# Attention sums spread by a matmul and inverted in the values' layout, in a conv-attention-lookup block on one core

## The chip, the cores and the metric

The kernel runs on one core of a Trainium2 chip. The metric is the time on the device of one execution in microseconds (us): of the kernel before, the median of three runs.

## The reference, cut to what matters

`x` is a (2, 128, 16, 16) tensor. It is group-normalised and goes through a decaying scan over its 128 channels; the sum with `x` is read as 2 x 256 tokens of 128 features. Then comes attention with 8 heads of 16 dimensions and a recency bias, and last a table-like integer lookup that tests some channels of each token and adds one-hot vectors:

```python
x = x + _L0_conv_ref(_gn(x), ...)
t = _to_tokens(x)                                  # 2 x 256 x 128
# attention
qkv = jnp.einsum('bsh,oh->bso', _ln_t(t), w_qkv)
attn = jnp.einsum('bhqd,bhkd->bhqk', q, k) / math.sqrt(hd)
bias = jnp.where(pos <= 0, pos * math.log(0.9), 0.0)
attn = jax.nn.softmax(attn + bias, axis=-1)
out = jnp.einsum('bhqk,bhkd->bqhd', attn, v).reshape(batch, seq_len, hidden)
t = t + jnp.einsum('bsh,oh->bso', out, w_out) + b_out
# lookup: bits of the normalised token select a shift of an 8-bit value
t = t + _L1_ffn_ref(_ln_t(t))
```

## The kernel before

Every engine has one program written out by hand; each step waits for named semaphores and raises one. There is no scheduler: an engine runs its steps strictly in the order of the code, so the calls at the ends of the `scalar`, `vector` and `tensor` blocks and the loops of the `gpsimd` block set the order.

Up to about 16 us the normalisation, the scan and the first projections run. Then comes attention. Its 2 batches x 8 heads are 16 heads, in four groups `g` of four (`HG`), two groups to a batch. A head goes through these steps:

- `scores_by_query(h)` (TensorE): scores with queries on the partitions, 2 products of 256 columns, into one of two PSUM buffers `s1_ps`. `largest(h)` (VectorE) takes each query's largest, `L741`; the next use of that buffer, by head `h + 2`, waits for it. Behind the fourth head of a group, `largest` also writes the negative maxima as two fp16 parts, `mparts` (`L748`, `L749`).
- `shift_rows(g)` (TensorE) transposes `mparts`; `even_shifts(g)` (ScalarE, `L477`) and `odd_shifts(g)` (VectorE, `L664`) copy the rows into spare rows of `qT`, so that the next product includes the shift.
- `scores_by_key(h)` (TensorE, `L975`, `L977`): the scores again with keys on the partitions, shifted, and `exponentials(c)` (ScalarE, `L496`) for two heads at once, 1,024 columns.
- `values(g, t)` (TensorE, `L994`): the product with `v_aug`. The output `pv_ps[g]` is 128 x 256 in fp32: each head has a block of 32 partitions (`VW`), 16 dimensions, then the sum of the exponentials (a column of ones in `v_aug`), then zeros; the 256 columns are queries. The four heads use four column blocks of the array. `pv_ps` of groups 0 to 2 is one PSUM bank, so the products of the next group wait until that bank has been read.
- `by_query(g)` (VectorE, `L671`) transposes 32x32 blocks, so that a query's sum is one column in each block of 32; `invert(g)` (`L675`) takes the reciprocal of 8 columns; GpSimd multiplies (`L344`, `L352`); `by_dim(g)` (VectorE, `L679`) transposes back into `oT`.
- `project(b)` (TensorE, `L1010`): four fp32 products of a batch's two groups with `woutT`; `residual(b)` and `token_stats(b)` (VectorE, `L685` to `L692`) add and take statistics; `token_scale` (ScalarE), `find_channels`, `look_up`, `one_hots` (VectorE, `L698` to `L732`), the fields `hot` (GpSimd) and `plus_normalised` (ScalarE) form the lookup, and `output(b)` transposes.

`keep_warm` issues products of zeros (`L814`) that nothing reads. GpSimd also writes the constants in its spare time, then `t1b` and `second_lows(t)` (`L307`): copies that the transposes of the stacks of queries and keys (`transpose_stacks`, `L916`) wait for.

Of the kernel before, what the change touches and what calls it, by code (L numbers as in the profile page):

```python
# [15 lines left out]
P = 128  # L16
# [18 lines left out]
WARM_X, WARM_Z, WARM_SCAN, WARM_MAX, WARM_PV, WARM_OUT = 9, 1, 5, 2, 8, 7  # L35
# [5 lines left out]
def conv_attn_ffn(nc, x, log_A, dt_w, dt_b, ln_w, ln_b, w_qkv, w_out, b_out, out):  # L41
# [3 lines left out]
    with ExitStack() as ctx:  # L45
# [199 lines left out]
        def _(pool):  # L245
# [84 lines left out]
            link(pool.tensor_scalar(ident2[:], ident16[:], 2.0, 0.0, ALU.mult, ALU.add), s=s_consts)  # L330

# [10 lines left out]
            for g in range(NG - 1):  # L342
                pool.wait_ge(s_rsum, g + 1)
                pool.tensor_tensor(on[:, g, :, :], pvq[:, g, :, :],  # L344
                                   rsum[:, g, :].unsqueeze(2).broadcast_to([P, HW // VW, VW]), ALU.mult)\
                    .then_inc(s_on, 1)

            for b in range(B):
                ts = slice(HALVES * b, HALVES * (b + 1))
                if b == 1:  # L350
                    pool.wait_ge(s_rsum, NG)
                    pool.tensor_tensor(on[:, NG - 1, :, :], pvq[:, NG - 1, :, :],  # L352
                                       rsum[:, NG - 1, :].unsqueeze(2).broadcast_to([P, HW // VW, VW]), ALU.mult)\
                        .then_inc(s_on, 1)
                pool.wait_ge(s_frs, b + 1)
                link(pool.tensor_scalar(neg_frs[:, ts], frs[:, ts], -1.0, 0.0, ALU.mult, ALU.add),
                     pool.tensor_scalar(one_frs[:, ts], frs[:, ts], 1.0, 0.0, ALU.add, ALU.add))
                pool.tensor_tensor(neg_fm[:, ts], fmv[:, ts, 0], neg_frs[:, ts], ALU.mult).then_inc(s_nfm, 1)
                pool.wait_ge(s_above, b + 1)
                link(pool.tensor_scalar(lift[:, ts], above[:, ts, SHL], 0.5, 0.5, ALU.mult, ALU.add))  # L360
                pool.tensor_tensor(hot[:, ts, :, :], hot_at[:].unsqueeze(1).broadcast_to([P, HALVES, 2, D]),
                                   lift[:, ts].unsqueeze(2).unsqueeze(3).broadcast_to([P, HALVES, 2, D]), ALU.mult)\
                    .then_inc(s_hot, 1)
# [445 lines left out]
        def _(pe):  # L809
# [171 lines left out]
            def values(g, t):  # L981

                b = g // 2
                if g == NG - 1:
                    pe.wait_ge(s_mre, NG)
                    pe.wait_ge(s_mro, NG)
                elif g > 0:
                    pe.wait_ge(s_pvq, g)
                else:
                    pe.wait_ge(s_odd, NG - 1)  # L990
                    pe.wait_ge(s_even, NG - 1)
                pe.wait_ge(s_exp, 2 * g + 2)
                for j in range(HG):
# [124 lines left out]
```

## Time and profile before

| | |
|---|---|
| runs | 54.54, 54.62, 56.0 us; median 54.62 |
| the profiled execution | 54.57 us, of it 52.8 us span |
| busy in the span | TensorE 41.4 us (78%), VectorE 41.0 (78%), ScalarE 28.7 (54%), GpSimd 22.1 (42%) |
| granted TensorE clock | 1.00 |
| the chain that ended last | TensorE 51% of the span, VectorE 24%, ScalarE 13%, waiting for nothing shown 5%, GpSimd 1% |

The span runs from the first to the last instruction; 1.8 us of the time lie outside it. Busy shares average over stages of different kinds. The chain is followed back from the last instruction, at each step to what released it, so its shares tell in which engine's hands the end lay.

### The profile page before, as it was taken

The numbers are of one execution on the slowest core, as the hardware profiler recorded it, in microseconds if no ns is written. First come the engines' busy times: TensorE is split into PE (matmuls) and PEld (weight loads), VectorE is DVE, ScalarE is ACT, GpSimd is POOL, SyncE is SP. The second block draws the span as 40 slices with busy tenths as digits, with TensorE's granted clock in tenths as the row PEclk, the third lists the DMA queues.
The fourth block names the chain that finished last, engine by engine and source line by source line (L and its number), as shares of the span: only waits on it lengthen the run. The fifth ranks groups of instructions, "written<-read, shape, count | busy, mean of one in ns | idle before, by whom it ended". The sixth has DMA issues, their size and how long they took to land.

```text
span 52.8 us, 1024 instructions
## 1 busy us (share of the span) xinstructions
PE 41.4 (78%) x317; PEld 26.1 (49%) x317; DVE 41.0 (78%) x136; ACT 28.7 (54%) x63; POOL 22.1 (42%) x62
## 2 busy tenths in 40 slices
PE   0999999199993989717994997899996399996710
PEld 0331988073521765315861594389664246841500
DVE  2699577859868279999979999998899964599620
ACT  3500476397392599806999239609839910045120
POOL 4788323099999886993000004021009304007000
PEclk9999999999999999999999999999999999999999
DMA  0482300000000000000000000000000000002002
GB/s 0 88 283 50 33 3 0 0 0 0 0 0 0 6 0 0 6 19 0 0 0 0 0 0 0 0 0 0 0 12 0 0 0 0 0 0 86 13 0 99
DMA packets 1565, 0.92 MB, mean 17 GB/s; under 512 B 404, under 2 KB 1560, under 8 KB 1560
## 3 DMA queue, kind: packets, MB, share of 16 engines
q1 hardware_dynamic: 1104, 0.79, 5.0%
q10 hardware_dynamic: 456, 0.08, 1.5%
q8 instruction: 2, 0.03, 0.3%
q14 instruction: 3, 0.02, 0.2%
HBM read 0.60 MB, written 0.26 MB: 16 GB/s over the span
## 4 chain that ended last, share of the span: by engine, by line
PE 51%; DVE 24%; ACT 13%; issue 5%; POOL 1%; DVEq 0%; ACTq 0%
PE ps L814 13%; PE ps L994 8%; ACT probs L496 8%; DVE negmax L741 6%; PE ps L975 5%; PE ps L1010 4%; PE ps L977 3%; PE ps L916 3%; PE ps L944 3%; DVE stacks L660 3%; PE ps L840 2%; PE ps L894 2%; ACT parts L435 2%; DVE xt L627 1%; DVE parts L648 1%
## 5 line engine op out<-in xcount | busy, mean ns | idle before, releaser
L814 PE MATMUL ps<-warm 128*128 128x512 bf16 x35 | 10.8, 444 | 1.3 <-DVE warm L541 1.3
L741 DVE TENSOR_REDUCE negmax<-ps 128x2 f32<-128x512 f32 x16 | 10.7, 674 | 0.7 <-PE ps L944 0.6
L496 ACT ACTIVATE probs<-ps 128x1024 f32<-128x1024 f32 x8 | 8.0, 1021 | 3.9 <-PE ps L977 3.9
L344 POOL TENSOR_TENSOR on<-pvq,rsum 128x256 f32<-128x256 f32 x3 | 1.8, 615 | 14.1 <-DVE rsum L675 14.1
L975 PE MATMUL ps<-stacks 128*128 128x256 f16 x32 | 7.0, 273 | 0.0
L977 PE MATMUL ps<-qmk,ident 128*128 128x256 f16 (+1 forms) x32 | 6.6, 246 | 0.0
L814 PEld LDWEIGHTS ps<-warm 128*128 128x128 bf16 x35 | 3.6, 109 | 5.7 <-issue 2.6
L944 PE MATMUL ps<-stacks 128*128 128x256 f16 x32 | 6.0, 273 | 0.5 <-DVE negmax L741 0.3
L994 PE MATMUL ps<-probs,v_aug 128*32 128x256 f32 x64 | 4.3, 384 | 1.7 <-ACT probs L496 1.5
L944 PEld LDWEIGHTS ps<-stacks 128*128 128x128 f16 x32 | 2.4, 97 | 2.4 <-issue 1.6
L975 PEld LDWEIGHTS ps<-stacks 128*128 128x128 f16 x32 | 3.1, 98 | 0.8 <-ACT stacks L477 0.4
L994 PEld LDWEIGHTS ps<-probs,v_aug 128*32 128x32 f32 x64 | 1.9, 109 | 3.1 <-issue 2.0
L977 PEld LDWEIGHTS ps<-qmk,ident 128*128 128x128 f16 x32 | 3.1, 98 | 0.2
L483 ACT ACTIVATE fln<-fmv 128x2 f32<-128x2 f32 x2 | 0.4, 204 | 5.1 <-DVE fmv L692 5.1
L473 ACT COPY stacks<-ps 64x1024 f16<-64x1024 f16 x3 | 3.0, 1007 | 0.3 <-PE ps L916 0.3
L894 PE MATMUL ps<-wT,xtT 128*128 128x384 f32 x8 | 3.0, 496 | 0.1
L958 PE MATMUL ps<-ident,mparts 128*128 128x128 f16 x8 | 1.1, 224 | 2.1 <-DVE mparts L749 2.1
L916 PE MATMUL ps<-ident,parts 128*128 128x128 f16 x32 | 2.3, 219 | 0.3 <-POOL parts L307 0.3
L679 DVE STREAM_TRANSPOSE oT<-on 128x256 f32<-128x256 f32 x4 | 1.8, 443 | 0.9 <-POOL on L352 0.7
L477 ACT COPY stacks<-ps 64x512 f16<-64x512 f16 x4 | 2.3, 580 | 0.3 <-PE ps L958 0.2
L544 DVE MEMSET stacks<- 64x1024 uint32 x2 | 1.8, 912 | 0.5 <-issue 0.5
L916 PEld LDWEIGHTS ps<-ident,parts 128*128 128x128 f16 x32 | 1.8, 97 | 0.8 <-POOL parts L307 0.5
(157 smaller groups left out, 92.5 us busy)
## 6 DMA issues: line engine op xcount, KB each, us to landing
x_sb<-in_x_dram SPq DMA_DIRECT2D x1, 256.0 KB, 2.9
out_dram<-y_sb SPq DMA_DIRECT2D x2, 128.0 KB, 1.7
wqkv_sb<-in_L_attn_w_qkv_dram SPq DMA_DIRECT2D x1, 192.0 KB, 3.0
wout_sb<-in_L_attn_w_out_dram SPq DMA_DIRECT2D x1, 64.0 KB, 3.3
bout_bc<-in_L_attn_b_out_dram ACTq DMA_DIRECT2D x1, 64.0 KB, 4.1
params<-in_L_conv_ln_w_dram ACTq DMA_DIRECT2D x1, 1.0 KB
params<-in_L_conv_ln_b_dram ACTq DMA_DIRECT2D x1, 1.0 KB
params<-in_L_conv_dt_w_dram ACTq DMA_DIRECT2D x1, 0.5 KB
```

What stands on the lines that cost most here:

```text
L473: act.copy(group_stacks(g, 0)[0:P // 2], stacks_ps[g][0:P // 2]).then_inc(s_even, 1)
L477: act.copy(qT.rearrange("p (a e) t -> p a e t", e=2)[P // 2:P, 2 * (g % 2):2 * (g % 2) + 2, 0, HW * (g // 2):HW * (g // 2 + 1)], mT_ps[P / ...
L496: act.activation(probs[:, 2 * c:2 * c + 2, :, :].rearrange("p h k q -> p (h k q)"), s2_ps[c % 2].rearrange("p a n -> p (a n)"), ACT.Exp, s ...
L741: dve.tensor_reduce(negmax[:, g, :, quadrant], s1_ps[h % 2].rearrange("p (q k) -> p q k", q=HALVES), AX_X, ALU.max, negate=True).then_inc( ...
L814: pe.matmul(ps[:, bank, :], warm[:, 0:P], warm[:], start=True, stop=True)
L894: pe.matmul(qkv_ps[:, t, 0:3 * P], xtT[:, P * t:P * (t + 1)], wT[:, 0:3, :].rearrange("p k h -> p (k h)"), start=True, stop=True).then_inc ...
L916: last = pe.transpose(stacks_ps[g][:, o, a, P * t:P * (t + 1)], parts[:, 2 * b + t, o, h:h + 2, :, :] .rearrange("p h i d -> p (h i d)"), ...
L944: last = pe.matmul(s1_ps[h % 2][:, HW * t:HW * (t + 1)], qT[:, e, HW * b + P * t:HW * b + P * (t + 1)], kT[:, e, HW * b:HW * (b + 1)], sta ...
L975: pe.matmul(dst, kT[:, e, HW * b + P * t:HW * b + P * (t + 1)], qT[:, e, HW * b:HW * (b + 1)], start=True, stop=False)
L977: last = pe.matmul(dst[:, P * t:HW], ident16[:], qmk[:, 0:HW - P * t], start=False, stop=True)
L994: last = pe.matmul(pv_ps[g][VW * j:VW * (j + 1), :], v_aug[:, 2 * b + t, HG * (g % 2) + j, :], probs[:, HG * g + j, t, :], start=(t == 0), ...
L1010: last = pe.matmul(proj_ps[b][:, t, :], oT[:, 2 * b + g, P * t:P * (t + 1)], woutT[:, g, :], start=(g == 0), stop=(g == 1))
```

## The change

The sum of a head's exponentials stays where the values product leaves it, in row 16 of the head's block of 32 partitions. A group's 128 x 256 block is copied to SBUF (`copy_values`: ScalarE for groups 0, 1 and 3, VectorE for group 2). A new step of TensorE, `spread_sums(g)`, multiplies it with a constant matrix `spread` that copies row 16 of each block onto its 32 rows; the result `sums_ps[g]` has the sum of each query under every value. VectorE takes the reciprocal of all 256 columns (`normalise`), GpSimd multiplies (VectorE for group 3), and the product is `oT` without a transpose. `spread` is written by two more instructions of GpSimd among its constants.

Beside that: `odd_shifts(1)` and `(2)` go from VectorE to ScalarE; `values(g, c)` goes by pairs of heads and not by halves of the keys, so that it can start on one exponential; `project(1)` is in two halves around `spread_sums(3)`, and the residual and the statistics of the last batch go tile by tile; eight fillers (`WARM_PV`) in front of `project(1)` go; `token_scale(0)` stands behind the last copy of values, and `hot_fields(0)` on GpSimd ahead of group 2's product. Queries 12 to 14 stand ahead of values of group 1.

```diff
-WARM_X, WARM_Z, WARM_SCAN, WARM_MAX, WARM_PV, WARM_OUT = 9, 1, 5, 2, 8, 7
+WARM_X, WARM_Z, WARM_SCAN, WARM_MAX, WARM_OUT = 9, 1, 5, 2, 7
...
-        pvq = sb("pvq", [P, NG, HW // VW, VW])
-        rsum = sb("rsum", [P, NG, HW // VW])
-        on = sb("on", [P, NG, HW // VW, VW])
+        pv_sb = sb("pv_sb", [P, NG, HW])
+        rsum = sb("rsum", [P, NG, HW])
+        spread = sb("spread", [P, P])
...
+        sums_ps = [ps[:, bank, HW:2 * HW] for bank in (6, 6, 6, 7)]
...
+            link(pool.memset(spread[:], 0.0), s=s_consts)
+            blocks = spread[:].rearrange("p (j w) -> p j w", w=VW)
+            link(pool.affine_select(out=blocks, in_=blocks, compare_op=ALU.not_equal, fill=1.0, base=-HD,
+                                    pattern=[[-VW, HG], [0, VW]], channel_multiplier=1), s=s_consts)
...
+            for g in range(NG - 1):
+                if g == NG - 2:
+                    hot_fields(0)
+                pool.wait_ge(s_rsum, g + 1)
+                pool.tensor_tensor(oT[:, g, :], pv_sb[:, g, :], rsum[:, g, :], ALU.mult).then_inc(s_oT, 1)
...
+            def copy_values(g):
+                act.wait_ge(s_pv, g + 1)
+                act.copy(pv_sb[:, g, :], pv_ps[g]).then_inc(s_pvc, 1)
...
             for g in range(1, NG):
                 even_shifts(g)
-                if g == NG - 1:
-                    token_scale(0)
+                if g < NG - 1:
+                    odd_shifts(g)
+                    copy_values(g - 1)
                 exponentials(2 * g)
                 exponentials(2 * g + 1)
+            copy_values(NG - 1)
+            token_scale(0)
...
-            def by_query(g):
-
-                dve.wait_ge(s_pv, g + 1)
-                dve.transpose(pvq[:, g, :, :].rearrange("p a w -> p (a w)"), pv_ps[g]).then_inc(s_pvq, 1)
-
-            def invert(g):
-                dve.wait_ge(s_pvq, g + 1)
-                dve.reciprocal(rsum[:, g, :], pvq[:, g, :, HD]).then_inc(s_rsum, 1)
-
-            def by_dim(g):
-                dve.wait_ge(s_on, g + 1)
-                dve.transpose(oT[:, g, :], on[:, g, :, :].rearrange("p a w -> p (a w)")).then_inc(s_oT, 1)
+            def copy_values():
+                dve.wait_ge(s_pv, NG - 1)
+                dve.tensor_copy(pv_sb[:, NG - 2, :], pv_ps[NG - 2]).then_inc(s_pvc2, 1)
+
+            def normalise(g):
+                dve.wait_ge(s_sums, g + 1)
+                dve.reciprocal(rsum[:, g, :], sums_ps[g]).then_inc(s_rsum, 1)
+                if g == NG - 1:
+                    dve.wait_ge(s_rsum, g + 1)
+                    dve.wait_ge(s_oT, g)
+                    dve.tensor_tensor(oT[:, g, :], pv_sb[:, g, :], rsum[:, g, :], ALU.mult).then_inc(s_oT, 1)
...
             def residual(b):
 
+                if b == 1:
+                    for t in tiles(1):
+                        dve.wait_ge(s_proj, t)
+                        dve.wait_ge(s_t1b, t + 1)
+                        dve.tensor_tensor(t2[:, t, :], proj_ps[1][:, t - HALVES, :], t1b[:, t, :], ALU.add)\
+                           .then_inc(s_t2, 1)
+                        dve.wait_ge(s_t2, t)
+                        dve.bn_stats(fst[:, t, :], t2[:, t, :]).then_inc(s_fst, 1)
...
+            def values(g, c):
...
+                pe.wait_ge(s_exp, 2 * g + c + 1)
+                for t in range(HALVES):
+                    for j in range(2 * c, 2 * c + 2):
+                        last = pe.matmul(pv_ps[g][VW * j:VW * (j + 1), :],
+                                         v_aug[:, 2 * b + t, HG * (g % 2) + j, :], probs[:, HG * g + j, t, :],
+                                         start=(t == 0), stop=(t == HALVES - 1))
...
+            def spread_sums(g):
+                if g == NG - 2:
+                    pe.wait_ge(s_pvc2, 1)
                 else:
+                    pe.wait_ge(s_pvc, min(g + 1, NG - 1))
+                if g == 0:
+                    pe.wait_ge(s_consts, 12)
+                elif g < NG - 1:
+                    pe.wait_ge(s_rsum, g)
+                pe.matmul(sums_ps[g], spread[:], pv_sb[:, g, :], start=True, stop=True).then_inc(s_sums, 1)
...
+            def project(b, groups=range(2)):
...
+                                     start=(g == 0), stop=(g == 1), skip_group_check=True)
+                    if b == 1 and g == 1:
+                        last.then_inc(s_proj, 1)
+                if b == 0:
+                    last.then_inc(s_proj, 1)
...
+            scores_by_query(12)
+            shift_rows(2)
+            scores_by_query(13)
+            scores_by_query(14)
+            values(1, 0)
+            values(1, 1)
+            scores_by_query(15)
+            scores_by_key(8)
+            scores_by_key(9)
...
             values(2, 0)
-            values(2, 1)
             for h in range(HG * (NG - 1), HG * NG):
                 scores_by_key(h)
+            values(2, 1)
             values(3, 0)
+            spread_sums(2)
             values(3, 1)
-            keep_warm(WARM_PV, 2)
-            project(1)
+            project(1, [0])
+            spread_sums(3)
+            project(1, [1])
             output(0)
```

GpSimd, the last of its constants. Names are those of tensors, written<-read; in brackets the semaphores that a row waits for. Before:

```order
L330 TENSOR_SCALAR ident2<-ident16 128x128 [waits consts]
L332 MEMSET eq2 128x288 [waits consts]
L338 TENSOR_TENSOR t1b<-t1,bout_bc 128x128 [waits t1_ready,bout_in]
L338 TENSOR_TENSOR t1b<-t1,bout_bc 128x128
L338 TENSOR_TENSOR t1b<-t1,bout_bc 128x128 [waits t1_ready]
L338 TENSOR_TENSOR t1b<-t1,bout_bc 128x128
L307 COPY parts<-parts 128x2x8x16 [waits lo_ready] x2
```

After:

```order
L333 TENSOR_SCALAR ident2<-ident16 128x128 [waits consts]
L334 MEMSET spread 128x128 [waits consts]
L336 AFFINE_SELECT spread<-spread 128x128 [waits consts]
L339 MEMSET eq2 128x288 [waits consts]
L345 TENSOR_TENSOR t1b<-t1,bout_bc 128x128 [waits t1_ready,bout_in]
L345 TENSOR_TENSOR t1b<-t1,bout_bc 128x128
L345 TENSOR_TENSOR t1b<-t1,bout_bc 128x128 [waits t1_ready]
L345 TENSOR_TENSOR t1b<-t1,bout_bc 128x128
L310 COPY parts<-parts 128x2x8x16 [waits lo_ready] x2
```

Two instructions for `spread` stand between `ident2` and `eq2`, ahead of `t1b` and of the copies of `second_lows(2)` and `(3)`.

VectorE, from `largest(9)` on; `pvq` is what `by_query` writes, and each `TENSOR_REDUCE` is a `largest`. Before:

```order
L741 TENSOR_REDUCE negmax<-ps 128x2 [waits s1_done]
L671 STREAM_TRANSPOSE pvq<-ps 128x256 [waits pv_done]
L741 TENSOR_REDUCE negmax<-ps 128x2 [waits s1_done]
L675 RECIPROCAL rsum<-pvq 128x8 [waits pvq_ready]
L741 TENSOR_REDUCE negmax<-ps 128x2 [waits s1_done]
L748 TENSOR_SCALAR mparts<-negmax 128x8 [waits max_ready]
L749 SCALAR_TENSOR_TENSOR mparts<-negmax,mparts 128x8 [waits dve_step]
L741 TENSOR_REDUCE negmax<-ps 128x2 [waits s1_done]
L679 STREAM_TRANSPOSE oT<-on 128x256 [waits on_ready]
L664 COPY stacks<-ps 64x2x256 [waits mT_done]
L741 TENSOR_REDUCE negmax<-ps 128x2 [waits s1_done]
L671 STREAM_TRANSPOSE pvq<-ps 128x256 [waits pv_done]
```

After, from `largest(8)` on (x4: four in a row):

```order
L772 TENSOR_REDUCE negmax<-ps 128x2 [waits s1_done] x4
L779 TENSOR_SCALAR mparts<-negmax 128x8 [waits max_ready]
L780 SCALAR_TENSOR_TENSOR mparts<-negmax,mparts 128x8 [waits dve_step]
L694 RECIPROCAL rsum<-ps 128x256 [waits sums_spread]
L772 TENSOR_REDUCE negmax<-ps 128x2 [waits s1_done] x4
L779 TENSOR_SCALAR mparts<-negmax 128x8 [waits max_ready]
L780 SCALAR_TENSOR_TENSOR mparts<-negmax,mparts 128x8 [waits dve_step]
L694 RECIPROCAL rsum<-ps 128x256 [waits sums_spread]
L684 COPY stacks<-ps 64x2x256 [waits mT_done]
```

The transposes are gone. `normalise(0)` stands between `mparts` of group 2 and `largest(12)`, `normalise(1)` behind `mparts` of group 3, and the third odd shift behind it.

TensorE, from the last values product of group 3 to the end of `project(1)`. Before:

```order
L994 MATMUL ps<-probs,v_aug 32x256 [waits exp_done,odd_shifts,even_shifts]
L994 MATMUL ps<-probs,v_aug 32x256 x3
L994 MATMUL ps<-probs,v_aug 32x256 [waits exp_done,odd_shifts,even_shifts]
L994 MATMUL ps<-probs,v_aug 32x256 x3
L814 MATMUL ps<-warm 128x512 x8
L1010 MATMUL ps<-woutT,oT 128x128 [waits oT_ready,t2_ready,max_ready]
L1010 MATMUL ps<-woutT,oT 128x128 [waits oT_ready] x3
```

After, with `values(2, 1)` ahead of `values(3, 0)` no longer shown:

```order
L1018 MATMUL ps<-probs,v_aug 32x256 [waits exp_done,odd_shifts,even_shifts]
L1018 MATMUL ps<-probs,v_aug 32x256 x3
L1033 MATMUL ps<-pv_sb,spread 128x256 [waits sums_inverted,third_values_copied]
L1018 MATMUL ps<-probs,v_aug 32x256 [waits exp_done]
L1018 MATMUL ps<-probs,v_aug 32x256 x3
L1045 MATMUL ps<-woutT,oT 128x128 [waits oT_ready,t2_ready,max_ready]
L1045 MATMUL ps<-woutT,oT 128x128 [waits oT_ready]
L1033 MATMUL ps<-pv_sb,spread 128x256 [waits values_copied]
L1045 MATMUL ps<-woutT,oT 128x128 [waits oT_ready,t2_ready,max_ready]
L1045 MATMUL ps<-woutT,oT 128x128 [waits oT_ready]
```

The fillers are gone; `spread_sums(2)` stands ahead of `values(3, 1)`, and `spread_sums(3)` between the halves of `project(1)`.

## Rows read from the trace of the kernel before

**Rows 1.** Windows: stretch, length; busy us of PE, PEld, DVE, ACT, POOL; PEclk, DMA, GB/s.
```profile
29.00:37.50 8.50, 8.00 (x87) 5.82 (x88) 8.04 (x20) 4.93 (x6) 1.23 (x2) 1.00 0.00 0
37.50:41.80 4.30, 2.95 (x37) 1.95 (x38) 4.06 (x18) 3.16 (x7) 1.74 (x6) 1.00 0.02 4
```

**Rows 2.** The chain that ended last, in order of time: start us, us, work.
```profile
23.90 0.41 POOL parts L307
...
24.35 0.62 PE ps L916 x8
```

**Rows 3.** Timeline of GpSimd: start us, us, work, [idle before <-releaser].
```profile
0.80 0.20 POOL L256 MEMSET ident<- 128x128 f32 x1 [0.29 <-POOLq L1104]
...
2.03 0.53 POOL L262 TENSOR_SCALAR_AFFINE_SELECT group_avg<-group_avg 128x128 f32<-128x128 f32 x1
...
2.62 0.52 POOL L264 TENSOR_SCALAR_AFFINE_SELECT group_avg<-group_avg 128x128 f32<-128x128 f32 x1
...
23.42 0.88 POOL L307 COPY parts<-parts 128x256 f16<-128x256 f16 x2
```

**Rows 4.** Groups of VectorE by line: count | busy us, mean ns | idle before.
```profile
L741 DVE TENSOR_REDUCE negmax<-ps 128x2 f32<-128x512 f32 x16 | 10.7, 674 | 0.7 <-PE ps L944 0.6
...
L671 DVE STREAM_TRANSPOSE pvq<-ps 128x256 f32<-128x256 f32 x4 | 1.8, 445 | 0.5 <-PE ps L994 0.5
...
L685 DVE TENSOR_TENSOR t<-ps,t1b 128x256 f32<-128x256 f32 x2 | 0.8, 425 | 0.6 <-PE ps L1010 0.5
...
L675 DVE RECIPROCAL rsum<-pvq 128x8 f32<-128x8 f32 x4 | 0.8, 196 | 0.1
...
L721 DVE TENSOR_TENSOR mask<-mask_at,active 128x4 uint32<-128x4 f32 x2 | 0.3, 154 | 0.0
```

**Rows 5.** Timeline of TensorE.
```profile
19.21 1.46 PE L894 MATMUL ps<-wT,xtT 128*128 128x384 f32 x4
...
29.02 1.07 PE L994 MATMUL ps<-probs,v_aug 128*32 128x256 f32 x16 [0.22 <-DVE stacks L660]
...
30.02 0.39 PE L944 MATMUL ps<-stacks 128*128 128x256 f16 x2
...
31.02 0.38 PE L944 MATMUL ps<-stacks 128*128 128x256 f16 x2
...
31.23 0.27 PE L975 MATMUL ps<-stacks 128*128 128x256 f16 x1
...
32.00 0.38 PE L944 MATMUL ps<-stacks 128*128 128x256 f16 x2
...
32.71 0.29 PE L958 MATMUL ps<-ident,mparts 128*128 128x128 f16 x2 [0.33 <-DVE mparts L749]
...
36.35 1.11 PE L1010 MATMUL ps<-woutT,oT 128*128 128x128 f32 x8
```

**Rows 6.** Timeline of ScalarE.
```profile
12.40 0.37 ACT L424 COPY wT<-ps 128x256 f32<-128x256 f32 x1
...
31.21 2.01 ACT L496 ACTIVATE probs<-ps 128x1024 f32<-128x1024 f32 x2 [1.81 <-PE ps L977]
...
33.25 0.58 ACT L477 COPY stacks<-ps 64x512 f16<-64x512 f16 x1
```

**Rows 7.** Timeline of several engines in the tail.
```profile
43.75 0.61 POOL L352 TENSOR_TENSOR on<-pvq,rsum 128x256 f32<-128x256 f32 x1 [2.23 <-DVE rsum L675]
...
45.65 0.42 DVE L685 TENSOR_TENSOR t<-ps,t1b 128x256 f32<-128x256 f32 x1 [0.50 <-PE ps L1010]
...
46.62 1.69 PE L814 MATMUL ps<-warm 128*128 128x512 bf16 x7
...
46.63 0.25 DVE L692 BATCH_NORM_AGGREGATE fmv<-fst 128x2 f32<-128x6 f32 x2
...
48.74 0.17 DVE L719 SCALAR_TENSOR_TENSOR idx<-first,flip 128x6 uint32<-128x6 uint32 x1
...
48.83 0.78 PE L1022 MATMUL ps<-ident,t 128*128 128x128 f32 x4 [0.53 <-ACT t L490]
```

More of the change, by code:

```diff
@@ L340, in _, with hot_fields @@
             second_lows(3)
[L342 to L348, printed above, removed]
-                ts = slice(HALVES * b, HALVES * (b + 1))
[L350 to L358, printed above, removed]
+            def hot_fields(b):
+                ts = slice(HALVES * b, HALVES * (b + 1))
                 pool.wait_ge(s_above, b + 1)
@@ L363, in _ @@
                     .then_inc(s_hot, 1)
+            for g in range(NG - 1):
[3 more added lines that the diff above has]
+                pool.tensor_tensor(oT[:, g, :], pv_sb[:, g, :], rsum[:, g, :], ALU.mult).then_inc(s_oT, 1)
+            for b in range(B):
+                ts = slice(HALVES * b, HALVES * (b + 1))
+                pool.wait_ge(s_frs, b + 1)
+                link(pool.tensor_scalar(neg_frs[:, ts], frs[:, ts], -1.0, 0.0, ALU.mult, ALU.add),
+                     pool.tensor_scalar(one_frs[:, ts], frs[:, ts], 1.0, 0.0, ALU.add, ALU.add))
+                pool.tensor_tensor(neg_fm[:, ts], fmv[:, ts, 0], neg_frs[:, ts], ALU.mult).then_inc(s_nfm, 1)
+                if b == 1:
+                    hot_fields(b)
         @block.scalar
@@ L979, in scores_by_key @@
                     last.then_inc(s_s2, 1)
-            def values(g, t):
+            def values(g, c):
                 b = g // 2
[L984 to L988, printed above, removed]
-                else:
[L990 to L993, printed above, removed]
-                    last = pe.matmul(pv_ps[g][VW * j:VW * (j + 1), :],
-                                     v_aug[:, 2 * b + t, HG * (g % 2) + j, :], probs[:, HG * g + j, t, :],
-                                     start=(t == 0), stop=(t == HALVES - 1))
-                if t == HALVES - 1:
-                    last.then_inc(s_pv, 1)
@@ L1000, in project @@
-            def project(b):
+                if c == 0:
+                    if g == NG - 1:
+                        pe.wait_ge(s_mre, NG)
+                        pe.wait_ge(s_mro, NG)
+                    elif g > 0:
+                        pe.wait_ge(s_pvc, g)
+                    else:
+                        pe.wait_ge(s_odd, NG - 1)
+                        pe.wait_ge(s_even, NG - 1)
+                pe.wait_ge(s_exp, 2 * g + c + 1)
[4 more added lines that the diff above has]
+                                         start=(t == 0), stop=(t == HALVES - 1))
@@ L1001, in project @@
+            def project(b, groups=range(2)):
                 if b == 0:
                     pe.wait_ge(s_max, B * HEADS - 1)
-                    steps = [(t, g) for t in range(HALVES) for g in range(2)]
+                    steps = [(t, g) for t in range(HALVES) for g in groups]
                 else:
@@ L1006, in project @@
                     pe.wait_ge(s_t2, 1)
-                    steps = [(t, g) for g in range(2) for t in range(HALVES)]
+                    steps = [(t, g) for g in groups for t in range(HALVES)]
                 for t, g in steps:
@@ L1010, in project @@
                     last = pe.matmul(proj_ps[b][:, t, :], oT[:, 2 * b + g, P * t:P * (t + 1)], woutT[:, g, :],
-                                     start=(g == 0), stop=(g == 1))
-                last.then_inc(s_proj, 1)
+                                     start=(g == 0), stop=(g == 1), skip_group_check=True)
+                    if b == 1 and g == 1:
+                        last.then_inc(s_proj, 1)
+                if b == 0:
+                    last.then_inc(s_proj, 1)
             def output(b):
```

67 lines of the change are left out of this document (37 added, 30 removed).

## The prediction

> **What bounds the kernel now.** I read the chain that ended last first, since shares of busy time say little here: VectorE and TensorE are both over nine tenths busy from 29 to 37.5 us [rows 1]. The chain [rows 2] shows at 23.90 us that GpSimd's copy in `second_lows(3)` releases TensorE's transposes of the third stack group at 24.35, and that everything up to the values products of the first group at 29.02 [rows 5] hangs on them. From there TensorE's own queue carries the chain, broken by two exponentials per group. So three things can move the end: what delays GpSimd before 24 us, what lengthens TensorE's queue from 29 us on, and the row of steps behind the last exponential: values, sums, division, projection, residual. The last is serial: no engine has other work that could be late instead.
>
> The profiled execution took 54.57 us, 52.8 of them span; the median is 54.62, so sums against 54.57 hold for it.
>
> **Part 1: the matrix `spread` on GpSimd.** A memset and an `affine_select` are put ahead of the memset of `eq2`, in a queue with no gap up to `second_lows(2)` at 23.42 [rows 3]. Likes of both stand at the start: a 128x128 memset 0.20 us and a two-dimensional select 0.53, each with a 0.06 gap before the next [rows 3]: 0.85 us. `second_lows(2)` starts at 24.27, and (3) right behind it ends at 25.15 instead of 24.31. TensorE waits for exactly that, so 0.83 of it reach 29.02: **values(0) starts at 29.85**. Nothing between hides it: TensorE already sat idle before 24.35, and VectorE and ScalarE next wait for TensorE. If one dimension makes the select cheaper, 0.6 remains.
>
> **Part 2: what a 256-column reciprocal costs.** This is the term that decides. Before, `invert` takes 8 columns in 196 ns on average, while a VectorE operation on 4 columns takes 154 [rows 4], thus some 150 fixed. Two readings: the surplus is fixed, and 256 columns cost what the addition of 256 from PSUM costs, 0.43 us [rows 4]; or it is per column, (196-150)/8 = 5.75 ns, and 256 columns cost 0.15 + 1.47 = **1.62 us**. I take the second: at one column per cycle 8 columns add under 10 ns to an operation, as 4 against 256 show ((425-154)/252 = 1.1 ns each), and nothing else about this instruction, whose input is a column taken from each block of 32, explains five times that. Its ends are 0.43 and, with the slowest surplus I can read from the row's rounding, 1.8.
>
> The Trainium skill ("VectorE: DVE Perf Modes", First, the fixed hardware budget) says that reciprocal is an iterative divide "with a repeat count of 8". At eight steps for every column one reciprocal would be an estimated 2.3 us and the sum 63.5; the row of 8 columns is about 20 ns too short for that, so the rule is taken for its sign, and the row for the size.
>
> **Part 3: 29 to 39 us.** Steps of TensorE's queue by start-to-start [rows 5]: values of one group 1.00 us, one query score 0.21, a pair of key scores 0.77, the row transposes 0.12 (their 0.29 less the drain of 0.17, which a pair of queries shows as 0.38 less 0.21). `spread_sums` is an fp32 product of 256 columns; two fp32 projections of 384 columns took 1.46, 1.29 without the drain [rows 5], 1.68 ns a column, so 0.43 each. ScalarE gets odd shifts (as its even shifts, 0.58) and copies of values (as a 128x256 copy, 0.37) [rows 6]: per group 2.0 + 0.58x2 + 0.37 = 3.5 of a period over 4.3 us; it keeps up and costs nothing here. The DVE transposes go, 0.445 each [rows 4], from beside that queue.
>
> From 29.85: values 30.85, query 10, keys 4 and 5 31.85, query 11 32.06, spread_sums(0) 32.49, keys 6 and 7 33.26, query 12 33.48, shift and query 13 33.82. Query 14 writes over what `largest(12)` reads, and on VectorE `normalise(0)` stands ahead of `largest(12)`: behind `mparts` (33.3) it runs to 34.9, `largest(12)` takes 0.67 [rows 4] to 35.5. TensorE stands from 33.82 to 35.52, where its longest wait before was 0.33 [rows 5]. Behind query 14: values(1) 36.75, query 15 36.97, keys 37.74, spread_sums(1) 38.17, keys **38.94**. Before, this point is at 36.35 [rows 5]: 2.6 later, of which 0.83 are part 1, 0.86 the two spreads, 1.17 the reciprocal over the short reading, 0.5 the queries moved together, less 0.8 of old waits. `normalise(1)` waits for `largest(15)` and `mparts` (38.3), ends at 39.97; GpSimd multiplies for 0.61 [rows 7] to 40.65; three of the four products of project(0) wait for that and end at 41.40, residual(0) starts at 41.57.
>
> **Part 4: the tail.** values(2,0) uses two of the four column blocks: four products run at once in the 1.00 of [rows 5], here two, so it takes as long as a whole group. Keys 12 to 15 end at 43.94, values(2,1) and (3,0) together near 45.3. VectorE's residual(0) to the start of look_up is 3.09 long (45.65 to 48.74 for the second batch [rows 7]), then copies group 2's values, 0.42: 45.07. The rest is serial: spread_sums(2) to 45.73, drained 45.9; reciprocal to 47.5; GpSimd's product 48.2; project(1,[0]) 0.44, 48.7; spread_sums(3) 49.13, drained 49.3 (ScalarE's copy was done long before); reciprocal 50.95; VectorE's product about 0.42, 51.4; first half of project(1,[1]) 51.75. The halves save about 0.2: the first addition starts while the second product runs, but two additions and two statistics with a wait between each take 0.1 more than the joined ones. The first addition starts at 51.77, and the statistics end at 53.15 where before they end at 46.88 [rows 7]: **6.2 us later**. One-hots(0), token_scale(0) and the fields of GpSimd lie in the reciprocals' shadow; what stands behind the statistics is unchanged. The eight fillers that go stood in a wait of VectorE and GpSimd and cost nothing before. Sum: 54.57 + 6.2 = **60.8 us**.
>
> **Rivals.**
> (a) *The reciprocal is one column per cycle.* Four times 1.19 less, all four on the chain: 54.57 + 6.2 - 4.8 = 56.0 us, 55.0 to 57.0 with part 1 at 0.6, and with 0.4 more if half groups of values don't overlap. For it: the surplus is read from 8 columns only. Against: the size of that surplus. It decides at about 0.6 us a reciprocal.
> (b) *In between:* part of the surplus is fixed, the reciprocal costs 0.7 to 1.2: 57.2 to 59.4.
> (c) *Faster: VectorE sets the pace and is relieved.* It is 8.04 of 8.50 us busy from 29 to 37.5 [rows 1] and TensorE waits for its `mparts` at 32.71 [rows 5]. Four transposes (1.8) go there and two short reciprocals (0.9) come, and the tail loses two transposes (0.9) and 0.2 by the halves: -2.0, with part 1's 0.85 left -1.2: 53.4 us. It needs the short reciprocal and ScalarE, not VectorE, to be unimportant; against it, TensorE is 8.00 of 8.50 busy in the same stretch and gets two more products.
> (d) *TensorE's clock falls.* From 46 to 51.4 us it would have 1.9 us of work. The granted clock stayed at 1.00 (2.4 GHz) where it was busy 2.95 of 4.30 us [rows 1]; nothing as sparse is in the trace. At 1.2 GHz output(0) and the seven fillers, 45.65 to 48.31 now [rows 7], take 5.3 instead of 2.7, end at 57.2, and hold output(1), due at 48.83 + 6.2 = 55.0: 62.9 us. The skill ("TensorE: Matmul & The Clock Gate", What's actually happening) has the slow clock as the default that activity releases; no row here shows it fall.
>
> **How the numbers follow.** My forecast with its own range 59.5 to 62.3: 0.47; (d) 0.10; (b) 0.10; (a) 0.26; (c) 0.07. The likeliest is 60.8. From 55.6 to 63.0 leaves out (c), the lower part of (a) and little above: under 2 in 10. A change within 2% (about what can be told from none) ends at 55.7: about 0.4 of (a) and a little of (c), 0.13; faster 0.06; slower 0.81.
>
> **What would show each step.** Part 1: TensorE's third stack transposes at 25.2, not 24.35. Part 2: RECIPROCAL 128x256 at 1.6 us. Part 3: TensorE idle 1.7 before query 14, released by `largest(12)`; spread products 0.43 apart. Part 4: VectorE's two last reciprocals on the chain, and gaps of 2 us on TensorE before each half of project(1). I am wrong if the reciprocal is under 0.6 us, and too low if TensorE's clock drops.

## The result, and the profile after

| | before | after |
|---|---|---|
| runs | 54.54, 54.62, 56.0, 56.4; median 55.31 us | 65.01, 65.2, 65.74, 65.76; median 65.47 us |
| the profiled execution | 54.57 us | 65.76 us |
| its span | 52.8 us | 64.0 us |
| granted TensorE clock | 1.00 | 0.92 |

The ratio is 1.199, interval 1.184 to 1.213: slower, by 4.7 us more than the 60.8 that were forecast and 2.5 above 63.0, the top of the range. Some executions of every kernel here, before's 56.0 and 56.4 among them, are 1 us or more longer, and where one was profiled, attention mostly began 0.9 to 1.7 us later; the ratio leaves them out. The two profiled executions are 11.2 us apart, and these 11.2 are what the text accounts for.

The page of the kernel after, first the clock in 40 slices of 1.6 us, then the group of the new reciprocal (count | busy us, mean ns | idle before):

```profile
PEclk9999999999999999999999955899999998555599
...
L694 DVE RECIPROCAL rsum<-ps 128x256 f32<-128x256 f32 x4 | 7.0, 1756 | 3.5 <-PE ps L1033 3.5
```

Both halves of the story stand here. A 256-column reciprocal takes 1.756 us, above the 1.62 of the forecast. And the clock is at half in two places, which it never was in the profiled execution of before. The windows, in the columns of [rows 1]:

```profile
29.50:33.60 4.10, 4.08 (x44) 2.91 (x44) 3.56 (x7) 2.83 (x5) 0.00 (x0) 1.00 0.00 0
33.60:36.80 3.20, 1.43 (x20) 0.63 (x20) 2.94 (x4) 1.74 (x3) 0.72 (x1) 1.00 0.00 0
36.80:40.20 3.40, 3.40 (x19) 2.45 (x18) 1.60 (x4) 1.40 (x2) 0.00 (x0) 0.53 0.03 5
46.00:51.00 5.00, 3.04 (x26) 1.29 (x23) 3.15 (x10) 1.74 (x5) 1.11 (x4) 1.00 0.00 0
54.50:57.80 3.30, 3.00 (x12) 2.24 (x14) 2.26 (x11) 0.64 (x3) 0.47 (x3) 0.50 0.00 0
57.80:61.90 4.10, 3.72 (x14) 1.95 (x13) 1.90 (x12) 1.28 (x4) 0.61 (x3) 0.62 0.09 32
```

TensorE is busy 1.43 of the 3.20 us up to 36.8, and in the 3.40 after them it has the slow clock (0.53, most of it at 1.2 GHz), though it has work all the time. Where it is busy 3.04 of 5.00 (46 to 51) the clock stays. Experiment 4 shows the same sparse stretch once more, without a fall behind it.

GpSimd, what answers to [rows 3]; the last line is its product with the first reciprocal:

```profile
21.46 0.20 POOL L334 MEMSET spread<- 128x128 f32 x1
21.81 0.31 POOL L336 TENSOR_SCALAR_AFFINE_SELECT spread<-spread 128x128 f32<-128x128 f32 x1
...
24.11 0.74 POOL L310 COPY parts<-parts 128x256 f16<-128x256 f16 x2
34.82 0.72 POOL L361 TENSOR_TENSOR oT<-pv_sb,rsum 128x256 f32<-128x256 f32 x1 [9.97 <-DVE rsum L694]
```

TensorE, from the third stack transposes to the end ([rows 2, 5, 7]):

```profile
24.91 0.62 PE L938 MATMUL ps<-ident,parts 128*128 128x128 f16 x8 [0.95 <-POOL parts L310]
...
29.52 1.09 PE L1018 MATMUL ps<-probs,v_aug 128*32 128x256 f32 x16 [0.22 <-DVE stacks L680]
...
31.75 0.60 PE L1033 MATMUL ps<-pv_sb,spread 128*128 128x256 f32 x2
...
35.43 0.38 PE L966 MATMUL ps<-stacks 128*128 128x256 f16 x2 [1.77 <-DVE negmax L772]
...
38.47 1.17 PE L1033 MATMUL ps<-pv_sb,spread 128*128 128x256 f32 x2
...
42.29 0.94 PE L1045 MATMUL ps<-woutT,oT 128*128 128x128 f32 x6 [1.06 <-POOL oT L361]
43.16 1.06 PE L1018 MATMUL ps<-probs,v_aug 128*32 128x256 f32 x8
...
45.78 1.57 PE L1018 MATMUL ps<-probs,v_aug 128*32 128x256 f32 x16
...
48.07 1.06 PE L1018 MATMUL ps<-probs,v_aug 128*32 128x256 f32 x8
51.01 0.68 PE L1045 MATMUL ps<-woutT,oT 128*128 128x128 f32 x4 [1.89 <-POOL oT L361]
51.53 0.60 PE L1033 MATMUL ps<-pv_sb,spread 128*128 128x256 f32 x2
54.53 1.19 PE L1045 MATMUL ps<-woutT,oT 128*128 128x128 f32 x4 [2.40 <-DVE oT L698]
...
57.86 2.77 PE L836 MATMUL ps<-warm 128*128 128x512 bf16 x6 [0.33 <-issue]
```

The waits of 1.77, 1.89 and 2.40 us contain the reciprocals (the second also GpSimd's product, the third VectorE's) and stand where the forecast had them. Equal work shows the clock: `spread_sums` takes 0.60 at 31.75 and 1.17 at 38.47; half of `project(1)` takes 0.68 at 51.01 and 1.19 at 54.53; six recorded fillers take 2.77 us where seven took 1.69 [rows 7].

VectorE, in its order: the first reciprocal, `largest(12)` to `(14)` behind it, and the tail ([rows 4, 7]):

```profile
32.99 1.75 DVE L694 RECIPROCAL rsum<-ps 128x256 f32<-128x256 f32 x1
34.66 1.88 DVE L772 TENSOR_REDUCE negmax<-ps 128x2 f32<-128x512 f32 x3
...
46.96 0.43 DVE L690 COPY pv_sb<-ps 128x256 f32<-128x256 f32 x1 [0.69 <-PE ps L1018]
...
48.24 1.76 DVE L694 RECIPROCAL rsum<-ps 128x256 f32<-128x256 f32 x1 [0.33 <-PE ps L1033]
...
52.17 1.76 DVE L694 RECIPROCAL rsum<-ps 128x256 f32<-128x256 f32 x1 [1.88 <-PE ps L1033]
53.96 0.42 DVE L698 TENSOR_TENSOR oT<-pv_sb,rsum 128x256 f32<-128x256 f32 x1
55.34 0.29 DVE L706 TENSOR_TENSOR t<-ps,t1b 128x128 f32<-128x128 f32 x1 [0.95 <-PE ps L1045]
...
56.39 0.30 DVE L723 BATCH_NORM_AGGREGATE fmv<-fst 128x2 f32<-128x6 f32 x2
```

The statistics end at 56.69 against 46.88 before: 9.8 us, and 1.4 more come behind them. All four reciprocals are on the chain that ended last, three of them for their whole length, the first for 1.65 us:

```profile
33.09 1.65 DVE rsum L694
...
39.67 1.77 DVE rsum L694
...
48.24 1.77 DVE rsum L694
...
52.17 1.77 DVE rsum L694
```

### The profile page after: what moved, and what is told of

It is laid out like the page before. It is cut to its first block, busy times and chain, and to the rows that moved or that the text cites. A ratio compares the mean times of both kernels' runs of the same rounds, so it can differ in the third digit from the quotient of the medians.

```text
span 64.0 us, 1025 instructions
## 1 busy us (share of the span) xinstructions
PE 47.2 (74%) x315; PEld 29.4 (46%) x317; DVE 44.2 (69%) x129; ACT 31.2 (49%) x68; POOL 22.3 (35%) x63
## 4 chain that ended last, share of the span: by engine, by line
PE 46%; POOL 23%; DVE 21%; issue 6%; POOLq 0%; DVEq 0%
DVE rsum L694 11%; PE ps L836 11%; PE ps L1018 6%; PE ps L997 5%; PE ps L1045 4%; PE ps L1033 3%; PE ps L999 3%; POOL stacks L303 3%; DVE negmax L772 3%; POOL stacks L304 3%; PE ps L1060 3%; PE ps L966 3%; POOL t1b L345 3%; POOL parts L310 3%; POOL oT L361 2%
## 5 line engine op out<-in xcount | busy, mean ns | idle before, releaser
L772 DVE TENSOR_REDUCE negmax<-ps 128x2 f32<-128x512 f32 x16 | 10.7, 684 | 2.2 <-PE ps L966 2.1
L836 PE MATMUL ps<-warm 128*128 128x512 bf16 x25 | 9.8, 531 | 1.6 <-DVE warm L561 1.3
L694 DVE RECIPROCAL rsum<-ps 128x256 f32<-128x256 f32 x4 | 7.0, 1756 | 3.5 <-PE ps L1033 3.5
L361 POOL TENSOR_TENSOR oT<-pv_sb,rsum 128x256 f32<-128x256 f32 x3 | 2.2, 744 | 19.8 <-DVE rsum L694 19.8
L997 PE MATMUL ps<-stacks 128*128 128x256 f16 x32 | 8.2, 304 | 0.0
L966 PE MATMUL ps<-stacks 128*128 128x256 f16 x32 | 6.0, 274 | 2.3 <-DVE negmax L772 2.1
L1045 PE MATMUL ps<-woutT,oT 128*128 128x128 f32 x16 | 3.2, 334 | 5.4 <-POOL oT L361 3.0
L1018 PE MATMUL ps<-probs,v_aug 128*32 128x256 f32 x64 | 5.9, 385 | 0.2 <-DVE stacks L680 0.2
L1045 PEld LDWEIGHTS ps<-woutT,oT 128*128 128x128 f32 x16 | 2.5, 223 | 6.4 <-issue 5.1
L1033 PE MATMUL ps<-pv_sb,spread 128*128 128x256 f32 x8 | 3.1, 470 | 0.1
L496 ACT COPY pv_sb<-ps 128x256 f32<-128x256 f32 x3 | 1.1, 372 | 3.8 <-PE ps L1018 3.8
L507 ACT ACTIVATE t<-t,neg_fm,one_frs 128x128 f32<-128x128 f32 x4 | 1.8, 485 | 1.7 <-POOL neg_fm L368 1.6
```

Source lines behind the costliest of these rows:

```text
L361: pool.tensor_tensor(oT[:, g, :], pv_sb[:, g, :], rsum[:, g, :], ALU.mult).then_inc(s_oT, 1)
L694: dve.reciprocal(rsum[:, g, :], sums_ps[g]).then_inc(s_rsum, 1)
L772: dve.tensor_reduce(negmax[:, g, :, quadrant], s1_ps[h % 2].rearrange("p (q k) -> p q k", q=HALVES), AX_X, ALU.max, negate=True).then_inc( ...
L836: pe.matmul(ps[:, bank, :], warm[:, 0:P], warm[:], start=True, stop=True)
L966: last = pe.matmul(s1_ps[h % 2][:, HW * t:HW * (t + 1)], qT[:, e, HW * b + P * t:HW * b + P * (t + 1)], kT[:, e, HW * b:HW * (b + 1)], sta ...
L997: pe.matmul(dst, kT[:, e, HW * b + P * t:HW * b + P * (t + 1)], qT[:, e, HW * b:HW * (b + 1)], start=True, stop=False)
```

## Experiments

Profiles are compared from the start of the first values product, `v0`, to the end of the span, so that what lies ahead of attention plays no part: **before 23.8 us** (29.02 to 52.8), **after 34.5** (29.52 to 64.0). The run times are given beside it. Each figure "from v0" is that of one profiled execution.

**1. What a reciprocal costs by width.** The kernel before, with these on VectorE while it waits for x:

```diff
+            strided = ones[:].rearrange("p (a w) -> p a w", w=8)
+            for k, (dst, src) in enumerate([(probe[:, 0:2], ones[:, 0:2]), (probe[:, 0:8], ones[:, 0:8]),
+                                            (probe[:, 0:8], strided[:, 0:8, 0]), (probe[:, 0:32], ones[:, 0:32]),
+                                            (probe[:, 0:128], ones[:, 0:128])]):
+                dve.reciprocal(dst, src).then_inc(s_probe, 1)
...
+            dve.tensor_scalar(probe[:, 0:8], strided[:, 0:8, 0], 1.0, None, ALU.mult).then_inc(s_probe, 1)
```

> The kernel before with five reciprocals of 2, 8, 8 (every eighth column), 32 and 128 columns of ones and one 8-column multiplication, every eighth column too, on VectorE ahead of x's arrival; nothing reads them. If the cost is per column (6.3 ns, as 1.756 us for 256 columns gives with 0.15 fixed): 0.16, 0.20, 0.20, 0.35 and 0.96 us, and the strided multiplication 0.16. If the surplus on 8 columns came from the stride: 8 columns side by side take 0.16 and the strided multiplication 0.20. The time of the whole stays within 1% of before, since VectorE waits there.

Groups of VectorE, shapes apart (the two of 8 columns are the dense and the strided one):

```profile
L553 DVE RECIPROCAL probe<-ones 128x128 f32<-128x128 f32 x1 | 1.0, 953 | 0.0
...
L553 DVE RECIPROCAL probe<-ones 128x8 f32<-128x8 f32 x2 | 0.4, 203 | 0.1
...
L553 DVE RECIPROCAL probe<-ones 128x32 f32<-128x32 f32 x1 | 0.4, 353 | 0.0
...
L555 DVE TENSOR_SCALAR probe<-ones 128x8 f32<-128x8 f32 x1 | 0.2, 171 | 0.0
...
L553 DVE RECIPROCAL probe<-ones 128x2 f32<-128x2 f32 x1 | 0.2, 166 | 0.0
```

From 2 to 8, to 32, to 128 columns every step gives 6.2 to 6.3 ns a column ((953-353)/96 = 6.25); 128 to 256 gives (1756-953)/128 = 6.27 in the kernel after, from PSUM. It is per column, and on 8 columns the stride costs nothing. The expectation for the time of the whole fell: its single run took 57.72 us. The probes held VectorE until 5.96 us, 2.2 us past the start of its first work on x in before, and v0 came 3.1 us later.

**2. The division left out.** The kernel after, with a pass of the same shape in place of each reciprocal:

```diff
-                dve.reciprocal(rsum[:, g, :], sums_ps[g]).then_inc(s_rsum, 1)
+                dve.tensor_scalar(rsum[:, g, :], sums_ps[g], 1e-12, None, ALU.min).then_inc(s_rsum, 1)
```

> The changed kernel with the reciprocal of 256 columns replaced by a minimum with 1e-12, so the division by the sums is left out. Theory: the long reciprocal costs itself four times (1.76 against 0.43, 5.3 us) and, by the waits that it makes on TensorE, the clock (some 3.7 us): 56.5 us, granted clock 1.00 throughout. Rival: the clock falls because the eight fillers are gone, whatever the reciprocal takes: about 60 us, clock under 0.95.

Median 58.64 us (57.57 to 58.89), more than the 56.5 expected and less than the rival's 60; from v0 26.3. The two kernels are 10.7 us apart from v0 on (34.5 against 23.8), and 8.2 of these go with the reciprocals' length. TensorE now waits 0.55 before query 14 and 0.50 and 1.07 before the halves of `project(1)`, and from v0 to 56 us the clock is 0.99 on average, with no filler added. The missing fillers alone thus don't bring the clock down in this kernel: the long waits have to be there too.

**3. TensorE kept busy.** The kernel after, with products of zeros in its three long waits:

```diff
             scores_by_query(13)
+            pe.wait_ge(s_exp, 3)
+            keep_warm(7, 2)
             scores_by_query(14)
...
             values(3, 1)
+            keep_warm(8, 2)
             project(1, [0])
             spread_sums(3)
+            keep_warm(10, 2)
             project(1, [1])
```

> The changed kernel with 7 fillers in the wait ahead of query 14, 8 ahead of project(1,[0]) and 10 ahead of project(1,[1]). Theory: the clock holds at 1.00 and gives back the 1.9 us of 36.8 to 40.2 and some 1.8 at the end: 61.8 us; that is what the forecast left out. Rival: the fillers are in the way of what they stand before and the time stays at 65, though the clock holds.

Median 64.22 us (62.92 to 64.34), where 61.8 was expected; from v0 31.6, so **2.9 us** less than after. Windows, as above:

```profile
33.00:37.00 4.00, 3.69 (x28) 2.26 (x26) 3.64 (x7) 3.21 (x4) 0.72 (x1) 1.00 0.00 0
37.00:42.00 5.00, 3.95 (x42) 2.77 (x40) 4.03 (x7) 2.78 (x4) 0.33 (x1) 1.00 0.01 3
...
56.00:61.00 5.00, 3.23 (x19) 1.59 (x18) 3.41 (x19) 1.81 (x6) 1.09 (x5) 1.00 0.08 26
```

The reciprocals are as long as in after and the order is the same; beside the fillers only the clock differs. The second reciprocal starts 8.9 us behind v0 instead of 10.2, the statistics end 25.6 behind it instead of 27.2, and the stretch behind them takes 6.0 instead of 7.3. In after's profiled execution the slow clock thus cost in the middle (1.3 us) and in the tail (1.6). The shortest spans, 63.3 us of after and 61.1 of this kernel, are 2.2 us apart: 2.9 holds for the profiled pair, and is not a fixed price.

**4. The constants of `spread` later.** Their two instructions stand behind `second_lows(3)`, all else as in after.

> The changed kernel with GpSimd's two instructions for spread behind second_lows(3). Theory: TensorE's third stack transposes start at 24.35 instead of 24.91 and all behind them is 0.56 us earlier: 64.9 us. Rival: the wait for largest(12) or the clock's fall takes it up: 65.4.

v0 is at 29.02, as in before, against 29.52: part 1 is worth **0.50 us**. Median 64.52 us (63.26 to 64.82; 64.9 was expected); from v0 34.0, less than after's 34.5 by another half microsecond. TensorE and its windows:

```profile
34.94 0.38 PE L966 MATMUL ps<-stacks 128*128 128x256 f16 x2 [1.77 <-DVE negmax L772]
...
49.28 1.17 PE L1045 MATMUL ps<-woutT,oT 128*128 128x128 f32 x4 [1.89 <-POOL oT L361]
```

```profile
35.00:43.00 8.00, 6.50 (x62) 4.47 (x63) 5.44 (x13) 3.00 (x4) 1.18 (x2) 1.00 0.01 3
46.00:58.00 12.00, 7.38 (x31) 4.37 (x32) 7.53 (x24) 3.16 (x10) 2.42 (x9) 0.64 0.00 0
```

The wait before query 14 is as long as in after, 1.77 us, and the clock holds behind it (the spread product at 37.26 takes 0.65 us, not 1.17); it falls only in the tail, but there already by the first half of `project(1)` (1.17 us, where after took 0.68). The same order and the same wait thus cost clock in the middle of one execution and none in that of another: the long waits make a fall possible and don't fix where it comes. Another execution of this kernel has a span of 61.5 us where the profiled one has 63.0.

**5. Before without its eight fillers.** `keep_warm(WARM_PV, 2)` goes, nothing else.

> The kernel before without its eight fillers ahead of project(1). The forecast took them as costing and giving nothing: then 54.6 us and a granted clock of 1.00. Rival, after what the changed kernel's trace shows: without them TensorE has little work from 41.8 to 46 us, the clock falls there or behind, and project(1), output(0) and the seven later fillers run at half rate: 56 to 57 us.

Runs of 54.9 to 58.04 us, before's beside them 54.37 to 57.7. From v0 24.1 against 23.8, between no change and the rival's 56 to 57 us. The windows and the fillers behind `output(0)`:

```profile
43.50:46.60 3.10, 1.71 (x20) 1.02 (x20) 1.81 (x9) 0.64 (x2) 0.62 (x1) 1.00 0.00 0
46.60:52.00 5.40, 5.20 (x22) 3.20 (x23) 4.02 (x22) 1.54 (x5) 1.09 (x5) 0.68 0.07 24
```

```profile
48.59 2.76 PE L814 MATMUL ps<-warm 128*128 128x512 bf16 x6 [0.16 <-issue]
```

The clock falls here too, behind the last values products, and the whole is some 0.3 us longer: "cost nothing before" holds for the time in which they ran, not for what they kept.

**6. Experiment 2 with the tail filled** (3 fillers before the first half of `project(1)`, 4 before the second).

> The kernel of e2_no_recip (no division by the sums) with 3 fillers ahead of project(1,[0]) and 4 ahead of project(1,[1]). If the clock's falls come from the waits that the long reciprocal makes, there is nothing left for fillers to hold: as e2_no_recip, 57.6 us and within 0.3 of it from values(0) on. Rival: the fillers still help by 0.5 or more.

57.45 to 57.89 us, median 57.57, as expected; ratio 1.059 (1.051 to 1.067); clock 1.00 throughout the profiled execution, from v0 26.4. Against experiment 3, which differs in the division and the number of fillers, 5.2 us: **the reciprocals' own length**, 4 x (1.756 - 0.424) = 5.3. Against before 2.6 us are left that are neither clock nor division.

**7. The reciprocal as exp(-ln) on ScalarE**, constants late, tail filled:

```diff
+            def invert(g):
+                act.wait_ge(s_sums, g + 1)
+                link(act.activation(lsum[:, g, :], sums_ps[g], ACT.Ln))
+                act.activation(rsum[:, g, :], lsum[:, g, :], ACT.Exp, scale=-1.0).then_inc(s_rsum, 1)
```

> The changed kernel with the reciprocal taken as exp(-ln) on ScalarE (two passes of 256 columns, 0.37 us each, in the gaps between its exponentials), GpSimd's constants behind second_lows(3), and 3 and 4 fillers in the tail. If the reciprocal's length, the clock and GpSimd's order are the losses found so far (5.3, 2.9 and 0.5 us), what is left is the rest, some 2.5, plus 0.3 for each ScalarE passage on the chain: 57.5 to 58 us. Rival: without the reciprocal VectorE is so relieved that the new layout is worth what it was made for: 54.5 or less.

58.58 to 59.77 us, median 58.77; ratio 1.079 (1.071 to 1.087); from v0 27.8; 57.5 to 58 us were expected. Two passes of 0.38 and 0.42 us do what took 1.756, and with the later constants and the fillers the kernel gains 6.7 us over after. It is still slower than before, and 1.4 behind experiment 6: TensorE waits 0.99 for `oT` before the last products of `project(0)`, where ScalarE took an exponential ahead of the logarithm.

**8 to 10. The parts that should help, alone.** Before with the last projection in halves around six fillers and the residual tile by tile (8); with odd shifts 1 and 2 on ScalarE (9); with both (10).

```diff
-            keep_warm(WARM_PV, 2)
-            project(1)
+            project(1, [0])
+            keep_warm(6, 2)
+            project(1, [1])
```

> One part of the change alone, on the kernel before: project(1) in halves (the products of group 2 ahead of six fillers in place of eight, those of group 3 behind them), and residual and statistics of the last batch tile by tile. Two of four products leave the chain (0.45 us) and the first addition starts one product earlier (0.2), less 0.1 for more waits: 0.5 us faster, 54.1 against 54.6. Rival: what VectorE gains it loses in the four smaller steps, no change.

> One part alone: the odd shifts of groups 1 and 2 on ScalarE. If VectorE set the pace from 29 to 37.5 us, 0.33 us for each of two groups: 0.3 to 0.6 faster. If TensorE and the exponentials do, as the forecast has it, no change, or 0.3 slower where ScalarE's exponentials are moved back by 0.58.

> Both parts together on the kernel before: the sum of the two, 0.5 us faster if the odd shifts are worth nothing.

From v0 23.7, 23.8 and 23.8 us, as before's 23.8. With both, the ratio is 0.998 (0.995 to 1.001): no difference; of the other two alone the lowest runs, 54.58 and 54.56, lie among the lowest of before beside them (54.36 to 54.78), and no interval is on record for them. The 0.5 us expected of the halves did not come. TensorE and VectorE with both:

```profile
44.98 0.68 PE L1029 MATMUL ps<-woutT,oT 128*128 128x128 f32 x4 [0.20 <-DVE oT L688]
```

```profile
45.48 0.29 DVE L696 TENSOR_TENSOR t<-ps,t1b 128x128 f32<-128x128 f32 x1 [0.34 <-PE ps L1029]
...
46.53 0.30 DVE L713 BATCH_NORM_AGGREGATE fmv<-fst 128x2 f32<-128x6 f32 x2
```

The first addition comes 0.17 us earlier (45.48, 45.65 before [rows 7]) and the statistics end at 46.83 instead of 46.88: the two additions and two statistics, longer than the joined ones, take back most of what the early start gave.

**11. The query order undone** in experiment 6: values(1) ahead of query 14, keys 8 and 9 ahead of query 15.

> On e6_no_recip_filled (no division by the sums), one thing undone: values(1) ahead of query 14, keys 8 and 9 ahead of query 15, as before. If the queries moved together cost the wait for largest(12) and the rest of the middle is the two spread products: the wait of 0.5 us ahead of query 14 goes and 0.3 to 0.5 of the time with it, 57.1 us. Rival: largest(14) and (15) come later by as much, no change.

59.05 to 60.37 us, from v0 26.8, 0.4 more than in experiment 6. The expectation (57.1) fell: in this pair the change's order is a gain of 0.4 and not part of the loss. values(1) now takes 1.69 us instead of 1.08, since it starts before its second exponential is there. The run also makes values(1) wait for the first `rsum`, but the trace shows no wait of TensorE there. The other three spans are 57.6 to 58.5 us where experiment 6 has 55.7 to 55.9, and 1.7 to 2.8 us lie outside the spans instead of 1.8; why is open. The sign is clear, its size is not.

**12. Group 2 whole**, in experiment 6: values(2) in one piece ahead of keys 12 to 15, its copy ahead of `find_channels(0)`, `spread_sums(2)` ahead of values(3).

> On e6_no_recip_filled (no division by the sums), group 2 whole ahead of keys 12 to 15, its copy ahead of find_channels(0), spread_sums(2) ahead of values(3). In e6 two heads' half of values takes 1.06 us, as a whole group does, three times in the tail, and the copy waits for the second half. If that is the part of the 2.5 us that the tail holds, two halves run together again and sums, product and project(1,[0]) of group 2 are off the chain: 1.0 to 1.4 us less, 56.3 us. Rival: the end hangs on group 3 alone, and the time stays at 57.5.

56.42 to 58.15 us, the lowest near the 56.3 expected; from v0 25.4, **1.0 us less** than experiment 6. Two rows tell it, the end of the statistics in experiment 6 (v0 at 29.54) and here (30.81):

```profile
49.61 0.30 DVE L723 BATCH_NORM_AGGREGATE fmv<-fst 128x2 f32<-128x6 f32 x2
...
49.95 0.30 DVE L723 BATCH_NORM_AGGREGATE fmv<-fst 128x2 f32<-128x6 f32 x2
```

They end 19.4 us behind v0 instead of 20.4. In experiment 6 a half group took 1.06 us, as long as a whole one (1.09). Three things were moved at once, so the 1.0 us belongs to them together. Moving the first reciprocal behind `largest(14)` was not tried, since its input shares a PSUM bank with the next values.

No version was shown to be faster than before.

## Why the prediction was wrong, step by step

The direction and the largest term were right; the time was 4.7 us too low. The table uses the two profiled executions; against these the forecast of 6.2 us is 5.0 short. Their 11.2 us are, by the differences above:

| term | forecast | measured | from |
|---|---|---|---|
| constants of `spread` | 0.83 | 0.50 | v0, experiment 4 |
| reciprocals, over a short pass | 4.8 | 5.2 | experiments 3 and 6 |
| slow clock | 0 | 2.9 | after and experiment 3 |
| the rest | 0.6 | 2.6 | experiment 6 and before |

- **Part 1** named the right queue and the right wait; the select took 0.31 us, not 0.53, and the third stack transposes started at 24.91, not 25.2. The case for it stood in the text ("If one dimension makes the select cheaper, 0.6 remains").
- **Part 2** chose per-column over fixed, rightly: 6.25 ns a column against the 5.75 read from 8 columns. The row that it used had the answer within 8%; a probe of four widths settles it. The forecast also read the repeat count of 8 in the Trainium skill ("VectorE: DVE Perf Modes", First, the fixed hardware budget) as eight steps per column, an estimated 2.3 us; that reading doesn't agree with the 1.756 measured.
- **Part 3** forecast the wait before query 14 as 33.82 to 35.52; it ended at 35.43, from v0 5.9 us against 5.7. From 36.8 on the clock was low, keys 11 ended near 40.7 instead of 38.94, and `residual(0)` started at 43.26 instead of 41.57.
- **The step that failed** is the clock. The forecast put it in rival (d), with 0.10 and in the tail alone, "output(0) and the seven fillers", and took it as 1.00 in part 3 without a word on it; the one reason given, that the clock stayed at 1.00 where TensorE was busy 2.95 of 4.30 us [rows 1], says nothing of sparser stretches. Its own part 3 had TensorE standing 1.70 us between 33.82 and 35.52, a stretch sparser than any in rows 1; the rival wasn't asked there. What the runs showed in its place: with the waits filled the kernel takes 2.9 us less, 1.3 of it by the second reciprocal and 1.6 behind it (experiment 3). Where the rival did look, from 46 us on, the clock held through 51 and was at half from 54.5 on: output(0) and the fillers took 5.1 us (55.52 to 60.63), near its 5.3. The fall in the middle didn't have to come (experiment 4). With 2.9 more the sum would have been 63.7, still 1.8 under the median.
- **Parts 3 and 4 apart from the clock** were 2.0 us short. Experiment 3, where the clock holds, can be laid beside the forecast, both from v0: the second reciprocal starts at 8.9 us against 8.5, group 2's copy ends at 16.6 against 15.2, the statistics end at 25.6 against 23.3. Of these 2.3, 0.5 are the longer reciprocals. The largest piece, 1.0, lies between the second reciprocal and the copy, and there the forecast had a wait wrong: it let the copy follow VectorE's own steps from residual(0) on, while in the trace VectorE stands for 0.69 us before it (at 46.96) and is released by TensorE's values(2,1). The rest is spread over the handovers of the tail.
- **The 2.6 us** of the last row, which are neither clock nor division: undoing the halves of group 2, with its copy and its spread product, gives back 1.0 (experiment 12). The two spread products in the middle queue are some 0.9 by their length (0.43 each, as forecast), which no run isolates. About 0.7 is open.
- **"The halves save about 0.2"**: nothing (experiments 8 and 10). **Odd shifts on ScalarE** cost nothing, as forecast, and bring nothing (9).
- **Rivals (a), (b), (c)** needed a reciprocal under 1.2 us. With a short pass in place of the division and the clock held the kernel still took 57.57 us: (a), at 56.0, would have been 1.6 too low, and (c), the faster case, would not have come about either. The upper end of (b), 59.4, should be 59.1 by its own numbers (56.0 and four times 1.2 less 0.43).

## What to carry to other kernels

Before a small operation is widened to save the transposes around it, measure its price per column: here 8 columns at 0.2 us became 256 at 1.76, four times on the chain. A new wait of TensorE can cost twice, once for itself and once for the work behind it if the clock falls. Behind the same wait of 1.77 us it fell in one execution and held in another, so a forecast that finds such a stall should ask it for the clock, wherever it stands, and carry the answer as a range. And fillers that run in a wait are not worthless because they are free: what they are worth stands behind them.

## What was not expected of the hardware

- The clock went to 0.53 after a stretch in which TensorE was busy 1.43 of 3.20 us with one wait of 1.77, and in experiment 5 to 0.68 after 1.71 of 3.10. It held at 1.00 through 3.04 of 5.00, and in experiment 4 from 35 to 43 us, behind a wait of 1.77 us too. What decides between the two isn't shown.
- A values product of two of the four column blocks takes as long as one of four: 1.06 and 1.09 us.
- A reciprocal costs some 6.25 ns per column between 2 and 256 columns (from SBUF up to 128, from PSUM at 256), beside about 0.15 us fixed; 8 columns cost the same strided or not; logarithm and exponential of 256 columns on ScalarE take 0.80 together.
